# Moving the gate's product from GpSimd to VectorE, and half of a scan's summation from TensorE to GpSimd, in a two-layer kernel

## The reference

```
# token mixer: a selective scan, 64 states for each of 128 channels
def step(h, (u_t, d_t, b_t, c_t)):
    h = exp(d_t * A) * h + (d_t * u_t) * b_t        # the scan
    y = sum over the 64 states of h * c_t           # the C-products and their sum
# feed-forward: a shared expert, and 16 routed experts that take 512 tokens each per batch row
shared = (gelu(x Wsg) * (x Wsu)) Wsd
topk over the tokens for each expert;  eo = (gelu(xt Wg) * (xt Wu)) Wd * weight;  scatter-add
x = x + s * silu(shared + routed)
```

## Time and profile before

| | |
|---|---|
| median of 3 runs | 5485.1 us (5478.84 to 5487.81) |
| the profiled execution | 5497.09 us |
| its span, first to last instruction | 5495.0 us, mean granted PE clock 0.906 |
| busy PE / DVE / ACT / POOL | 4507.5 / 3718.0 / 2611.6 / 2795.8 us |
| drives on POOL, 512 | 1297.8 us |
| read_out on DVE, 512 | 615.6 us |
| sums into y on PE, 2048 records for 1024 matmuls | 1135.4 us |
| shared expert's stage | about 2250 to 3068 us |
| choosing stage | about 3068 to 3515 us |
| routed experts' stage | about 3515 to 5385 us |

### The profile page before, as it was taken

How to read it: one execution, slowest core, us unless ns; L and a number is a source line. 1 busy time by engine, 2 the same in 40 slices (tenths; PEclk the granted TensorE clock), 3 DMA queues, 4 the chain that set the end, 5 groups by cost and what they waited for, 6 DMA issues and landing times. The chain is left out here.

```text
span 5495.0 us, 62964 instructions
## 1 busy us (share of the span) xinstructions
PE 4507.5 (82%) x22290; PEld 3301.1 (60%) x22290; DVE 3718.0 (68%) x5054; ACT 2611.6 (48%) x4753; POOL 2795.8 (51%) x1941
## 2 busy tenths in 40 slices
PE   6799999878999996888888557688788778778872
PEld 5688888667888885556555325455555455555541
DVE  5466666554666663678877799777677677777765
ACT  5544444374444443655555212365555555555642
POOL 1100000120000002677677328789898999989982
PEclk8899999988999997889999668899899999899996
DMA  2000000110000001333333112344444444444447
GB/s 75 29 20 20 21 23 20 33 39 19 23 20 21 23 20 46 117 126 118 129 117 123 66 50 71 98 120 137 121 126 134 125 133 130 123 128 134 126 125 271
DMA packets 241482, 467.29 MB, mean 85 GB/s; under 512 B 33937, under 2 KB 153105, under 8 KB 241169
## 3 DMA queue, kind: packets, MB, share of 16 engines
q1 hardware_dynamic: 216592, 429.72, 23.6%
q0 software_dynamic: 24576, 33.57, 3.3%
HBM read 393.87 MB, written 69.34 MB: 84 GB/s over the span
## 5 line engine op out<-in xcount | busy, mean ns | idle before, releaser
L1323 POOL TENSOR_TENSOR scan_drive_sb<-scan_b_wide_sb,scan_du_sb 128x1024 f32<-128x1024 f32 x512 | 1297.8, 2542 | 264.4 <-DVE scan_h_sb L1244 254.8
L1244 DVE TENSOR_TENSOR_SCAN scan_h_sb<-decay_bank,scan_state_sb,scan_drive_sb 128x512 f32<-128x512 f32 x896 | 1123.6, 1272 | 399.8 <-ACT decay_bank L1489 378.3
L1409 PE MATMUL y_bank<-scan_ch_sb,identity_sb 128*128 128x512 f32 x2048 | 1135.4, 652 | 0.8 <-DVE scan_temp_sb L1257 0.8
L1489 ACT ACTIVATE decay_bank<-scan_delta_sb,a_neg_sb 128x512 f32<-128x512 f32 x1024 | 697.7, 684 | 317.9 <-DVE scan_h_sb L1244 316.5
L767 POOL TENSOR_TENSOR acc_b_sb<-acc_b_sb,g_in_b_sb 128x256 f32<-128x256 f32 x64 | 47.4, 741 | 1274.1 <-DVE acc_b_sb L750 1274.1
L824 PE MATMUL ybank<-v_low_hi_lo_sb,pt_hi_b_sb 128*128 128x384 f32 x2048 | 671.9, 361 | 20.1 <-DVE pt_lo_b_sb L714 15.9
L1251 DVE TENSOR_TENSOR scan_ch_sb<-c_pair,scan_h_sb 128x1024 f32<-128x1024 f32 x512 | 615.6, 1202 | 44.8 <-PE c_pair L1400 44.1
L714 DVE TENSOR_TENSOR pt_lo_b_sb<-pt,pt_hi_b_sb 128x512 fp32r<-128x512 f32 x512 | 353.2, 690 | 411.5 <-ACT pt_hi_b_sb L867 411.5
L1400 PE MATMUL c_pair<-scan_cc_sb,select_state_sb 128*128 128x512 f32 x1024 | 404.1, 479 | 256.8 <-DVE scan_ch_sb L1251 255.1
L825 PE MATMUL ybank<-v_low_hi_lo_sb,pt_lo_b_sb 128*128 128x256 f32 x2048 | 573.2, 280 | 0.0
L858 ACT ACTIVATE p_b_sb<-scores,softmax_cols_b_sb 128x1024 f32<-128x1024 f32 x256 | 286.3, 1118 | 539.3 <-DVE softmax_cols_b_sb L708 400.1
(11 more groups left out here) (317 smaller groups left out, 10617.4 us busy)
## 6 DMA issues: line engine op xcount, KB each, us to landing
scan_b_wide_sb<-b_scratch SPq DMA_DIRECT2D x512, 512.0 KB
x_b_sb<-x SPq DMA_DIRECT2D x16, 512.0 KB, 4.8
g_scratch<-g_out_b_sb SPq DMA_DIRECT2D x16, 512.0 KB, 3.2
x_res_b_sb<-x SPq DMA_DIRECT2D x64, 128.0 KB, 2.2
g_in_b_sb<-g_scratch SPq DMA_DIRECT2D x64, 128.0 KB, 2.2
x_scratch<-x_res_b_sb SPq DMA_DIRECT2D x64, 128.0 KB, 1.7
xn_scratch<-xn_out_b_sb SPq DMA_DIRECT2D x64, 128.0 KB, 1.7
scan_xn_sb<-xn_scratch SPq DMA_DIRECT2D x16, 512.0 KB, 4.1
```

What stands on the lines that cost most here:

```text
L1244: e.tensor_tensor_scan(k.h[i % H_BUFFERS][:, j, :], k.decay_banks[S % DECAY_BANKS][:, :], k.drive[i % DRIVE_BUFFERS][:, j, :], start, ALU. ...
L1323: e.tensor_tensor(k.drive[i % DRIVE_BUFFERS][:, :, :], k.b_wide[i % B_BUFFERS][:, :, :], k.du[c % 2][:, :].unsqueeze(1).broadcast_to([P, P ...
L1409: e.matmul(k.y_bank[:, :], consts.identity[:, :], k.ch[i % CH_BUFFERS][:, j, :], start=(n == 0), stop=(n == STATES - 1)).then_inc(k.s_y, 1)
L1489: e.activation(k.decay_banks[S % DECAY_BANKS][:, :], k.delta[c % 2][:, :], ACT.Exp, scale=wt.a[:, n:n + 1]).then_inc(k.s_decay, 1)
```

## The change

Three things change. The product `g = g * u` moves from POOL to DVE, in all groups and lists, at the same steps of the program. For the first 214 of 512 items POOL adds the two halves of `ch` in place (its new `read_out`), and PE adds one sum to y where it added two. From item 214 on the scan is as before. Whoever waited for a count of sums (DVE's read_out and the end of a chunk) counts by `additions`.

```diff
+SUMMED = 214
+def additions(items):
+    return max(0, min(items, SUMMED) + PAIR * (items - min(items, SUMMED)))
...
     def read_out(i):                                # DVE
...
-        w.wait_ge(k.s_y, PAIR * (i - CH_BUFFERS + 1))
+        w.wait_ge(k.s_y, additions(i - CH_BUFFERS + 1))
...
     def down(c):                                    # DVE
-        w.wait_ge(k.s_y, STATES * (c + 1))
+        w.wait_ge(k.s_y, additions(PAIRS * (c + 1)))
...
+    def read_out(i):                                # POOL
+        if i < SUMMED:
+            ch = k.ch[i % CH_BUFFERS]
+            w.wait_ge(k.s_ch, i + 1)
+            e.tensor_tensor(ch[:, 0, :], ch[:, 0, :], ch[:, 1, :], ALU.add).then_inc(k.s_ch_sum, 1)
...
     def add_up(S):                                  # PE
...
-        w.wait_ge(k.s_ch, i + 1)
         if n == 0:
             w.wait_ge(k.s_skip, c)
-        e.matmul(k.y_bank[:, :], consts.identity[:, :], k.ch[i % CH_BUFFERS][:, j, :], start=(n == 0), stop=(n == STATES - 1)).then_inc(k.s_y, 1)
+        if i >= SUMMED:
+            w.wait_ge(k.s_ch, i + 1)
+            e.matmul(k.y_bank[:, :], consts.identity[:, :], k.ch[i % CH_BUFFERS][:, j, :], start=(n == 0), stop=(n == STATES - 1)).then_inc(k.s_y, 1)
+        elif j == 0:
+            w.wait_ge(k.s_ch_sum, i + 1)
+            e.matmul(k.y_bank[:, :], consts.identity[:, :], k.ch[i % CH_BUFFERS][:, 0, :], start=(n == 0), stop=(n == STATES - PAIR)).then_inc(k.s_y, 1)
...
     def product(q):                                 # POOL: only h_lo is left
...
-            if f < HB:
-                w.wait_ge(k.s_gelu, HB * q + f + 1)
-                fills.wait_emptied(w, "moe_up", q, f, 1)
-                e.tensor_tensor(k.g[f][:, :], k.g[f][:, :], k.u[f][:, :], ALU.mult).then_inc(k.s_mult, 1)
             yield
...
+    def product(q):                                 # DVE
+        for f in range(HB):
+            w.wait_ge(k.s_gelu, HB * q + f + 1)
+            fills.wait_emptied(w, "moe_up", q, f, 1)
+            e.tensor_tensor(k.g[f][:, :], k.g[f][:, :], k.u[f][:, :], ALU.mult).then_inc(k.s_mult, 1)
+            yield
+        yield
```

More of the change, by code:

```diff
@@ L1076, in __init__ @@
         self.s_kept = self.sem("state_kept")
+        self.s_ch_sum = self.sem("ch_sum")
         self.s_y = self.sem("y_sum")
@@ L1346, in down @@
             e.tensor_tensor(out, out, wt.b_down[:, :].unsqueeze(1).broadcast_to([P, 2, D]), ALU.add).then_inc(k.s_bias, 1)
-    yield from scan_order(prepare, nothing, nothing, nothing, drive, nothing, nothing, nothing, nothing, nothing, down)
+    yield from scan_order(prepare, nothing, nothing, nothing, drive, nothing, nothing, read_out, nothing, nothing, down)
 def scan_tensor(e, w, k, fills, wt, consts):
@@ L2108, in choose @@
         yield
-    yield from moe_order(pace, shared_order(nothing, prepare_steps, turn, gate, up_steps, product_steps, down_steps), choose(),
-                         expert_order(nothing, nothing, gather_steps, turn, up_steps, product_steps, down_steps))
+    yield from moe_order(pace, shared_order(nothing, prepare_steps, turn, gate, up_steps, product, down_steps), choose(),
+                         expert_order(nothing, nothing, gather_steps, turn, up_steps, product, down_steps))
 def moe_tensor(e, w, k, fills, consts, pace):
```

## The result

The changed kernel takes 5591.84 us (median of 4 runs, 5588.45 to 5594.77) against 5485.02 us before: the ratio is 1.0194, with a 95% interval of 1.0179 to 1.0208. The forecast was 5419 us, with 5330 to 5520 as its range, so the time is 107 us longer and not 66 shorter, and lies 72 us outside the range. The profiled execution took 5594.77 us, its span 5593.1 us.

A forecast was written before the change was run, and what follows sets the result against it. PE was taken to lead the shared stage, VectorE the choosing stage, GpSimd the routed one. Terms -104 - 285 + 35 + 192p, with p (us per product on VectorE) 1.5, gave -66: 5419 us, range 5330 to 5520.

The forecast's parts named there:

- GpSimd's lateness: Routed experts' stage: late GpSimd delays ACT (354.9 us of waits), whose late decays leave VectorE idle (350.0 us).
- p = 1.5: Assumed price in us of each of the 192 products on VectorE, between bounds of 0.68 and 2.65.
- -285 + 128p: Routed experts' stage: change in us with 128 products at price p each; a gain of 93 at 1.5.
- the worst case: Product on VectorE held for one full GpSimd drive every time: 0.68 + 2.35 = 3.03 us, whole kernel below +228.
- forecast -8: Shared expert's stage: VectorE becomes longest, -104 us plus 64 products at 1.5 us each, a gain of 8.
- Neither is above 90% of its stage, so GpSimd paces neither: Shared and routed stages: with additions in and products out, GpSimd has 678 of 818 and 1557 of 1870 us.
- PE paces no longer: Shared expert's stage: 145 sums leave PE, 125 us, so its work falls from 692 to 567 us.
- PE's clock: Less work may lower PE's clock; with 567 us lengthened by a tenth PE stays under VectorE; no separate chance.
- The choosing stage: Additions delay drives, which then run against VectorE's compares: 17 us in the first half, 18 in the second, +35.
- The 22 additions there lie on a GpSimd that has been given 164 us back: Routed experts' stage: 22 additions of 1.28 us in the first lists, with no cost entered in the sum.
- The one on the port: Rival: GpSimd holds VectorE's products on SBUF; slower above 1.84 us each, +155 us at 2.65; chance 0.20.
- It balances: Rival: PE stands at the sum until GpSimd has added, losing 61 us, whole at -5; chance 0.10.

The follow-up runs named there:

- product_reduce: product_only with a tensor_reduce that copies u into g in place of VectorE's product, gate left out; 5295.92 us, ratio 0.9650.
- product_only: The changed kernel without the additions on GpSimd (SUMMED = 0), product still on VectorE; 5463.95 us, ratio 0.9954.
- product_drained: product_only with GpSimd waiting for its own result after each drive, low part of an expert's weights and h_lo; 5419.21 us, ratio 0.9871.
- idle_additions: The kernel before plus 214 GpSimd additions on a spare tile that no other engine waits for; 5608.85 us, ratio 1.0225.
- sums_both_matmuls: sums_only with both of PE's matmuls over the added half, so these items count twice in y; 5662.43 us, ratio 1.0321.
- sums_only: The changed kernel with the product back on GpSimd, 214 additions kept; 5625.91 us, ratio 1.0254.

## Why the prediction was wrong

**What bounds the kernel.** Right in the routed stage in that GpSimd's lateness went through ACT to VectorE: the two waits fell by 224 and 198 us. The time didn't follow, because the product on VectorE is itself held by what GpSimd is running. It had been ACT that waited for GpSimd; now VectorE did. The sentence that VectorE instructions "that read only SBUF wait for whatever GpSimd is doing" was too wide: a tensor_reduce that reads only SBUF was held in none of 192.

**The product's price.** The four stages together missed the forecast by 171 us, and 108 of them are the routed stage's (+15 in place of -93). So this is the larger step that failed: "about 1.2 with a GpSimd subtraction in the way ... I take p = 1.5". In the shared stage it was 1.26, in the routed one 2.36. The sum for that stage, -285 + 128p, gives +17 with 2.36, and the stage went by +15, so the mis-sized term was off by 128 x 0.86 = 110 us. That the sum comes out so near is in part luck: it puts nothing on the 22 additions, and with the tensor_reduce, p = 0.67, it gives -199 for this stage and -61 for the shared one, where product_reduce has -160 and -36. Neither bound was one: single products took up to 9.89 us, three times "the worst case" of 3.03, which took one drive as the longest hold, and those of block 1, the second of a list, have a mean of 3.73. A better estimate stood in the profile of the kernel before. The two lines that bounded p have means of 1.91 and 2.10 us there (the number behind the busy time, in ns):

```profile
L1228 DVE SCALAR_TENSOR_TENSOR scan_delta_sb<-scan_temp_sb 128x512 f32<-128x512 f32 x16 | 33.5, 2095 | 26.1 <-POOL scan_temp_sb L1310 26.1
L1224 DVE SCALAR_TENSOR_TENSOR scan_temp_sb<-scan_temp_sb 128x512 f32<-128x512 f32 x16 | 30.5, 1907 | 0.0
```

The 192 products had 2.00 in the changed kernel and 1.90 in product_only. What the runs put in the place of p = 1.5: a product is held by the GpSimd instruction under way, and behind an indirect DMA, where the records of GpSimd's instructions overlap, often over several. The Trainium skill, "SBUF — State Buffer", section "Who interferes with whom", says that the later one is blocked for the whole of the other. The trace agrees for 101 of the 129 held products and goes beyond it for 28. Why the overlap shuts a product out isn't shown; product_drained shows that with fewer such overlaps the long holds go.

**The shared stage.** Of the forecast -8, the product's share came out as -12 (product_only). What failed is "Neither is above 90% of its stage, so GpSimd paces neither" and "PE paces no longer": the additions cost +49 with the product on VectorE and +61 without. idle_additions has +52 with PE's sums left as before and no wait for the addition, so GpSimd's share of busy time was the wrong thing to ask. An addition can't begin before read_out, and the next drive stands behind it; before, that drive needed only the scan. PE's relief and PE's new wait for the addition nearly cancel: the stage is 899 us with neither (idle_additions), 940 with the wait alone (sums_both_matmuls) and 908 with both (sums_only), so the wait costs 41 and the relief gives back 32. How the 52 us divide between held instructions of VectorE (at most some 23), late drives and late products wasn't settled.

**PE's clock.** It was taken to cost nothing. In the shared stage PE was granted 1.2 GHz for 294 of 884 us, in the kernel before for 130 of 847. Behind some of PE's waits for an addition its matmuls run slower, and the timeline shows one case:

```profile
2603.78 1.69 PE L1427 MATMUL y_bank<-scan_ch_sb,identity_sb 128*128 128x512 f32 x2 [2.18 <-POOL scan_ch_sb L1338]
...
2605.70 0.63 PE L2185 MATMUL layer_bank<-moe_xt_lo_sb,Ws_uT_hi_sb 128*128 128x512 f32 x1
2606.12 0.63 PE L2186 MATMUL layer_bank<-moe_xt_hi_sb,Ws_uT_lo_sb 128*128 128x512 f32 x1
2606.55 0.63 PE L2184 MATMUL layer_bank<-moe_xt_hi_sb,Ws_uT_hi_sb 128*128 128x512 f32 x1
```

They start 0.43 us apart, against the 0.232 worked out in the prediction. The windows just ahead of the wait, behind it and a little later give the granted clock (the number behind the five engines):

```profile
2598.00:2601.00 3.00, 3.00 (x14) 2.28 (x13) 2.78 (x3) 1.47 (x4) 2.91 (x3) 1.00 0.32 91
2604.50:2607.40 2.90, 2.90 (x7) 1.91 (x6) 0.10 (x1) 0.00 (x0) 2.90 (x3) 0.50 0.13 20
2608.60:2610.00 1.40, 1.40 (x7) 1.18 (x7) 1.35 (x2) 0.64 (x2) 1.40 (x2) 1.00 0.15 59
```

That is 2.4, 1.2 and again 2.4 GHz. The 125 us of sums that were to leave PE became 50 us less busy (715.75 to 665.26 between the events). That the clock cost time of the whole isn't shown: in sums_both_matmuls, with the clock back at 0.88 and more matmuls, the stage was longer.

**The choosing stage.** The mechanism was right (addition in front, drive against VectorE's compares), the size too small: +53 against +35. The item of the bits shown above costs 2.0 us more, where 0.8 was taken; over the 17 items of bits and ranks it is 28/17 = 1.6 on average.

**The routed stage's additions.** "The 22 additions there lie on a GpSimd that has been given 164 us back" put them at nothing. By the scatters of the first and third lists they cost 14 to 22 us, with the product on VectorE and without.

**The rivals.** The one on the port named the right place, and its turn at 1.84 was passed; the average over both stages was (64 x 1.26 + 128 x 2.36)/192 = 1.99, which gives -354 + 192 x 1.99 = +28. The additions, which cost 128 us where the sum has 35 for them, make the rest of the +107. "It balances" named PE's wait for the sum, with 61 us for it; the wait alone came to 41. Each had been priced as if it came alone.

## What to carry over

Before an elementwise instruction goes from GpSimd to VectorE, look at its form, not only its length. In this kernel one with two inputs in SBUF, or a tensor_scalar from SBUF to SBUF, was held by GpSimd's instructions; one that reads PSUM and SBUF, or a tensor_reduce, wasn't. Its price depends on what GpSimd runs at that place (0.92 to 3.73 us for the four blocks), so take the mean of such lines in the profile of before (here 1.91 and 2.10 us, for a product that had 2.00), and look at the largest. And an instruction that is put into an in-order queue costs what comes late behind it as well (here the drive, which now stands behind read_out): 214 additions of 1.28 us, 274 us of work whose results nobody used, cost 120 us, most of it in stages where GpSimd had been busy 70% (shared), 26% and 79% of the time.

## What the runs showed of the hardware

- Behind an indirect DMA on GpSimd, the records of its instructions overlap by 0.6 us (a drive 2.95 us in place of 2.35), and a VectorE product with two inputs in SBUF was then held over up to five further ones, 9.89 us at the most. With a wait of GpSimd for its own result after each drive and low part, the holds over further instructions fell from 28 to 10 and the largest from 9.89 to 4.16 us; the kernel went from 5463.95 to 5419.21 us, 1.3% faster than before.
- In all 129 held products of the changed kernel the last 0.66 us, the length of an unheld one, begin 0.10 to 0.12 us before the record of a GpSimd instruction ends.
- A tensor_scalar of 128x512 with one input in SBUF (0.39 us at the least) was held as the product was; a tensor_reduce of the same size (0.65 to 0.69 us) in none of 192.
